# A fourth key tile for VectorE in six odd heads, its bias in the two groups that need it, and fourteen blocks in head 0

## The reference

```
query = x Wd_q Wu_q + rope(x Wd_q Wq_r)      key = x Wd_kv Wu_k + rope(x Wk_r)
value = x Wd_kv Wu_v                          (biases everywhere)
a     = softmax(query key^T / sqrt(272)) value, per head
x1    = layernorm(x + a Wo + b)
y     = round(x1 / s) (int8, s from the largest |x1|) times an int8 matrix, scaled, + bias
out   = layernorm(x1 + y)
```

## Time and profile before

| what | value |
|---|---|
| median of 3 runs | 1922.75 us (1921.45 to 1923.99) |
| profiled execution | 1922.54 us, its span 1920.7 us |
| busy share of the span | PE 96%, PEld 23%, DVE 82%, ACT 94%, POOL 9% |
| instructions of L909 | 1860, busy 1709.7 us |
| granted TensorE clock, mean | 0.99 |

### The profile page before, as it was taken

The page is one execution under the profiler, slowest core; times in us unless marked ns, Lnnn a source line. Parts: engine busy times, 40 slices in busy tenths (PEclk is TensorE's granted clock), DMA queues, the critical chain, the costliest instruction groups (busy, mean ns, idle before and its releaser), DMA issues.

```text
span 1920.7 us, 31434 instructions
## 1 busy us (share of the span) xinstructions
PE 1840.5 (96%) x12988; PEld 446.8 (23%) x12988; DVE 1583.1 (82%) x1502; ACT 1804.4 (94%) x2024; POOL 178.4 (9%) x132
## 2 busy tenths in 40 slices
PE   8989999999999999999999999999999999999965
PEld 3442222221221222222122222222222212221235
DVE  3868979988888887888888888888888888988577
ACT  3479999999999999999999999999999999999956
POOL 5645600000000000000000000000001000500010
PEclk9999999999999999999999999999999999999987
DMA  4534111111111011111121101111121101111012
GB/s 142 167 128 151 20 18 23 26 26 26 26 26 25 17 20 19 23 26 26 25 70 26 26 14 19 20 26 25 26 48 26 25 16 20 17 26 26 1 25 88
DMA packets 161383, 73.41 MB, mean 38 GB/s; under 512 B 129968, under 2 KB 146608, under 8 KB 160752
## 3 DMA queue, kind: packets, MB, share of 16 engines
q1 hardware_dynamic: 158224, 66.79, 15.1%
q10 hardware_dynamic: 3008, 4.53, 0.8%
HBM read 49.13 MB, written 20.84 MB: 36 GB/s over the span
## 4 chain that ended last, share of the span: by engine, by line
ACT 53%; PE 30%; issue 8%; DVE 7%; DMA 1%; POOL 0%; ACTq 0%; DVEq 0%; SPq 0%; POOLq 0%
ACT arena L909 52%; PE PS L708 14%; PE PS L658 9%; PE PS L1196 4%; DVE arena L969 2%; PE PS L749 1%; DVE arena L945 1%; DVE arena L955 1%; PE PS L1344 1%; ACT arena L869 0%; PE PS L1169 0%; DVE bn L837 0%; DVE arena L953 0%; DVE arena L965 0%; DMA arena<-arena 0%
## 5 line engine op out<-in xcount | busy, mean ns | idle before, releaser
L909 ACT ACTIVATE arena<-PS 128x1024 f32<-128x1024 f32 x1860 | 1709.7, 1278 | 10.4 <-PE PS L658 8.5
L708 PE MATMUL PS<-arena,Vh 128*32 128x512 f32 x8192 | 1091.5, 605 | 8.9 <-DVE arena L945 8.9
L658 PE MATMUL PS<-Qst,Kst 49*128 49x512 f16 x4096 | 717.5, 383 | 26.9 <-issue 4.6
L969 DVE SCALAR_TENSOR_TENSOR arena<-arena 128x2048 f32<-128x2048 f32 x282 | 645.5, 2289 | 0.1
L945 DVE TENSOR_SCALAR arena<-PS 128x512 int32<-128x512 f32 x376 | 259.5, 690 | 240.0 <-PE PS L658 235.5
L658 PEld LDWEIGHTS PS<-Qst,Kst 49*128 49x128 f16 x4096 | 183.6, 93 | 1030.6 <-ACT arena L909 982.9
L708 PEld LDWEIGHTS PS<-arena,Vh 128*32 128x32 f32 x8192 | 161.7, 108 | 328.5 <-issue 326.5
L965 DVE SCALAR_TENSOR_TENSOR arena<-arena 128x2048 f32<-128x2048 f32 x94 | 216.5, 2303 | 0.0
L953 DVE TENSOR_SCALAR arena<-arena 128x2048 int32<-128x2048 int32 x94 | 116.9, 1244 | 8.2
L955 DVE TENSOR_SCALAR arena<-arena 128x2048 int32<-128x2048 int32 x94 | 117.9, 1254 | 0.0
L1519 POOL TENSOR_SCALAR nmr<-mv 128x16 f32<-128x16 f32 x1 | 0.3, 263 | 1258.3 <-DVE mv L1698 1258.3
(11 more groups left out here) (120 smaller groups left out, 479.9 us busy)
## 6 DMA issues: line engine op xcount, KB each, us to landing
Qst<-q_halves SPq DMA_DIRECT2D x64, 128.0 KB
Kst<-k_halves SPq DMA_DIRECT2D x64, 128.0 KB
Vh<-head_values SPq DMA_DIRECT2D x30, 256.0 KB, 5.5
k_halves<-parts_or_sums SPq DMA_DIRECT2D x16, 256.0 KB, 3.1
q_halves<-parts_or_sums SPq DMA_DIRECT2D x16, 256.0 KB, 2.6
Qst<-q_halves SPq DMA_DIRECT2D x64, 64.0 KB
Kst<-k_halves SPq DMA_DIRECT2D x64, 64.0 KB
head_values<-arena SPq DMA_DIRECT2D x1, 4096.0 KB, 14.3
```

What stands on the lines that cost most here:

```text
L658: return nc.tensor.matmul(out, Kst[par][low:low + HK + 1, at:at + 128], Qst[par][low:low + HK + 1, j * CH:(j + 1) * CH], start=True, stop= ...
L708: last = nc.tensor.matmul(bank(value_bank(t))[32 * j:32 * j + 32, :], Vh[t % 2][:, kt, :], moving, start=kt == first, stop=kt == last_kt)
L909: nc.scalar.activation(ring(at, k), bank(g % SLOTS * SLOT, k), ACT.Exp, scale=EXP_SCALE).then_inc(a.exp, 1)
L969: last = nc.vector.scalar_tensor_tensor(out=t, in0=t, scalar=POLY[3 - j], in1=power if j == 3 else mantissa, op0=ALU.add, op1=ALU.mult)
```

## The change

It has five parts. (1) Key tile 14 goes to VectorE in heads 3, 7, 11, 15, 27 and 31: 100 tiles instead of 94, and 56 groups instead of 58 in those heads, 1848 in all. Since the values of one parity of heads share a buffer (Vh), tile 14's values and ones are stored times V_SCALE for all odd heads; in the odd heads in which ScalarE keeps tile 14 its two groups stand alone at the head's end and get a bias of -ln(V_SCALE). (2) The blocks are spread anew (BLOCKS_OF): 14 in head 0, 13 in heads 1 to 15 and 24 to 30, 12 in heads 16 to 23, 4 in the last. (3) Before attention three value products stand ahead of the last two query chunks; the key maximum's steps move between VectorE's steps; the table load moves behind first_shifts, into the evacuations; the first three score groups wait for their own banks and go ahead of the bias product; the addition of the output bias (first_sums) stands before the last query chunk's steps; and the wait for all of VectorE's steps at the fifth exponential becomes one for each part. (4) ffn_weights is spread over six blocks. (5) In the last norm GpSimd takes tiles 0 to 5 and 12 to 15 from ScalarE, and the first inverse deviations come two additions later.

```diff
@@ -35,14 +35,25 @@
+FOURTH, FOUR = 14, (3, 7, 11, 15, 27, 31)
+
+
 def by_vector(t):
 
-    return BY_VECTOR if t else FIRST_BY_VECTOR
+    return (FOURTH, *BY_VECTOR) if t in FOUR else BY_VECTOR if t else FIRST_BY_VECTOR
+
+
+def scaled(par):
+
+    return (FOURTH, *BY_VECTOR) if par else BY_VECTOR
 
 
 def head_blocks(t):
 
     low, high = ([kt for kt in half if kt not in by_vector(t)] for half in (range(UPPER), range(UPPER, KT)))
+    if FOURTH in low and t % 2:
+        low = [kt for kt in low if kt != FOURTH] + [FOURTH]
     both = min(len(low), len(high))
...
-FIRST_BLOCKS, FIRST_BLOCK = 13, 11
+FIRST_BLOCKS, FIRST_BLOCK = 14, 11
...
+BLOCKS_OF = [FIRST_BLOCKS] + [13 if t < 16 or t >= 24 else 12 for t in range(1, NT - 1)]
+BLOCKS_OF.append(QB * CYCLES - sum(BLOCKS_OF))
...
-        n = FIRST_BLOCKS if t == 0 else len(BY_VECTOR) * QB
-        n = min(n, QB * CYCLES - len(steps))
+        n = BLOCKS_OF[t]
...
-COPY_AFTER = {FIRST_BLOCKS - 1 + len(BY_VECTOR) * QB * t: t for t in range(NT - 1)}
+COPY_AFTER = {sum(BLOCKS_OF[:t + 1]) - 1: t for t in range(NT - 1)}
...
+EARLY_VALUES = 3
...
     for c in LATE:
+        if c == LATE[2]:
+            order += [("v", 0, n) for n in range(EARLY_VALUES)]
         order += [("p", c, QR_), ("p", c, UQ_), ("p", c, QHI)]
-    return order + [("v", 0, n) for n in range(KT // 2)]
+    return order + [("v", 0, n) for n in range(EARLY_VALUES, KT // 2)]
...
+            for g in range(SLOTS):
+                pe.wait_ge(s_ev, max(DONE[p] for p in PRODUCTS if PRODUCT_BANK[p] // SLOT == g))
+                scores(g)
+            pe.wait_ge(s_ev, len(PRODUCTS))
             bias_out()
-            for g in range(SLOTS):
-                scores(g)
...
+        def norm_by_gpsimd(tiles):
+            for t in tiles:
+                nc.gpsimd.tensor_scalar(Y[:, t, :], Y[:, t, :], rstd[:, t:t + 1], nmr[:, t:t + 1],
+                                        ALU.mult, ALU.add).then_inc(e_fp, 1)
...
-                if g == 4:
-                    act.wait_ge(s_dve, len(STEP))
-                nc.scalar.activation(ring(at, k), bank(g % SLOTS * SLOT, k),
-                                     ACT.Exp, scale=EXP_SCALE).then_inc(a.exp, 1)
+                if 4 <= g < 8:
+                    act.wait_ge(s_dve, STEP["low", LATE[g - 4], "q"])
+                if t % 2 == 1 and blocks[0][0] == FOURTH:
+                    nc.scalar.activation(ring(at, k), bank(g % SLOTS * SLOT, k), ACT.Exp, scale=EXP_SCALE,
+                                         bias=small[:, 9:10]).then_inc(a.exp, 1)
+                else:
+                    nc.scalar.activation(ring(at, k), bank(g % SLOTS * SLOT, k),
+                                         ACT.Exp, scale=EXP_SCALE).then_inc(a.exp, 1)
...
-            for first, end in ((0, 4), (4, 8), (8, 12), (12, 17)):
-                store(e_fa, end, first, end)
-            store(e_fa, 22, 17, 22)
+            store(e_fp, 4, 0, 4)
+            sp.wait_ge(e_fp, 6)
+            store(e_fa, 2, 4, 8)
+            store(e_fa, 6, 8, 12)
+            sp.wait_ge(e_fp, 10)
+            store(e_fa, 7, 12, 17)
+            store(e_fa, 12, 17, 22)
             store(e_fv, 3, 22, 25)
-            store(e_fa, 25, 25, 28)
+            store(e_fa, 15, 25, 28)
             store(e_fv, 6, 28, 31)
-            store(e_fa, 26, 31, KT)
+            store(e_fa, 16, 31, KT)
...
-                if p == ("v", 0, 8):
+                if p == ("v", 0, 10):
                     pe.wait_ge(s_kmax, 5)
...
+                        scales = [V_SCALE if kt in scaled(par) else 1.0 for par in range(2)]
+                        if scales[0] == scales[1]:
+                            last = nc.scalar.activation(V[:, :, kt, :], given, ACT.Copy, scale=scales[0])
+                        else:
+                            for par in range(2):
+                                last = nc.scalar.activation(V[:, par:H:2, kt, :], given[:, par:H:2, :], ACT.Copy, scale=scales[par])
...
-                if p == ("v", 0, 7):
+                if p == ("v", 0, 10):
                     first_shifts()
-            nc.scalar.activation(xs[:, 0:1], small[:, 6:7], ACT.Exp)
+                    nc.scalar.activation(xs[:, 0:1], small[:, 6:7], ACT.Exp)
...
             act.wait_ge(e_rs2, 2)
-            norm_by_scalar(e_fa, range(0, 6))
+            norm_by_scalar(e_fa, range(6, 12))
             act.wait_ge(e_mv2, 22)
             deviation(e_sd2, *BATCHES2[1])
-            norm_by_scalar(e_fa, range(6, 12))
             act.wait_ge(e_rs2, 4)
-            norm_by_scalar(e_fa, range(12, 16))
+            norm_by_scalar(e_fa, range(16, 20))
             act.wait_ge(e_mv2, 28)
             deviation(e_sd2, *BATCHES2[2])
-            norm_by_scalar(e_fa, range(16, 22))
+            norm_by_scalar(e_fa, range(20, 22))
...
+            pool.wait_ge(e_rs2, 2)
+            norm_by_gpsimd(range(0, 6))
+            pool.wait_ge(e_rs2, 4)
+            norm_by_gpsimd(range(12, 16))
...
+            def first_sums():
+
+                nc.vector.memset(sums_ok[:, :], 1.0).then_inc(s_sums, 1)
+                dve.wait_ge(s_bo, 1)
+                nc.vector.tensor_tensor(bo, PS[:, OT * CH:OT * CH + D], bo, ALU.add).then_inc(s_bo2, 1)
...
+                if (name, c, n) == ("low", NCH - 1, "k"):
+                    key_lengths(1)
                 if (name, c, n) == ("low", LATE[0], "q"):
-                    key_lengths(1)
-                if (name, c, n) == ("add", LATE[1], "q"):
                     key_row()
...
+                if (name, c, n) == ("low", LATE[2], "q"):
+                    first_sums()
...
-            hooks.update({40: check_range, 50: ffn_weights})
+            hooks.update({40: check_range})
+            hooks.update({50 + step: lambda step=step: ffn_weights(step) for step in range(6)})
...
-                    if 2 * g == end + 4:
+                    if 2 * g == end + (4 if b else 8):
```

55 lines of the change are left out of this document (29 added, 26 removed).

## The result

The changed kernel takes 1913.89 us (median of 6 runs, 1911.77 to 1917.94), the kernel before 1924.85 in the same comparison; the ratio is 0.9947, with an interval of 0.993 to 0.9965. So it gained 10.2 us (6.7 to 13.5) where 15.5 were forecast. The profiled execution took 1911.77 us, its span is 1910.0.

A forecast was written before the change was run, and what follows sets the result against it. ScalarE's exponentials were taken to bound the attention loop, with TensorE close behind. Start -2.5, loop -10.0 and tail -3.0 made -15.5 us, from 1922.75 to 1907.2; own range 1902 to 1911, wider 1900.5 to 1914.5.

The forecast's parts named there:

- the VectorE rival: Attention loop: VectorE becomes the bound, so the loop gives only -1 us and the total is 1916.2; chance 0.14.
- The twelve exponentials: Attention loop: six tiles moved to VectorE take 12 exponentials of 0.917 us off ScalarE's queue, -11.0 us.
- Head ends: Attention loop: first value products wait for bits at five head ends instead of ten, -3 us, bounds -5 and 0.
- Heads 0 and 1 under GpSimd: Attention loop: VectorE runs late where GpSimd adds the output bias, +2.5 us, bounds 0 and 5.
- Heads 27 and 28: Attention loop: VectorE's work in head 28 is 54.8 us against 53.2, +1 us, bounds 0 and 3.
- Head 3: Attention loop: a short head with the range check and three weight steps, late in places, +0.5 us, bounds 0 and 2.
- The start: Ahead of the loop: first exponential at 119.7 instead of 122.25, -2.5 us, bounds 0 and -3.5; shift-row transfer late next.
- The tail: Last norm: ten tiles go to GpSimd and the stores end sooner, -3.0 us, bounds -3.5 and +9.
- GpSimd's price: Last norm: time GpSimd needs per tile, taken as 0.7 us, up to about 2.8 if blocked; as a rival, chance 0.05.
- the rival in which it holds the stores: Last norm: GpSimd's ten tiles delay the stores, total 1927 at 2.8 us a tile; chance 0.05.
- TensorE as the bound: Attention loop: TensorE sets the pace, so the 12 exponentials bring nothing and the total is 1917.3; chance 0.08.

The follow-up runs named there:

- the second profile: The changed kernel itself run once more, with nothing edited, on the same chip: 1914.42 us, ratio 0.9948 to the kernel before.
- the tiles alone: The kernel before with only the fourth key tile, its blocks spread anew and the weight steps spread: 1923.83 us, ratio 0.9994.
- the kernel with the spreading: The changed kernel with GpSimd's output-bias additions spread over heads 0 to 15 and its FFN-bias additions over heads 28 to 31: 1906.59 us, ratio 0.9906.

## Why the prediction was right or wrong

The direction and the pacemaker were right. The time lies outside the forecast's own range of 1902 to 1911, in the upper end of the wider one of 1900.5 to 1914.5, and nearer to the VectorE rival's 1916.2 than to the forecast. The forecast itself was 6.7 us too low. 1.1 to 2.1 of these are the base: the sum was made against one execution of 1922.54 us and three runs around 1922.75, while the kernel before has a median of 1923.8 to 1924.9 over more runs. The rest is the loop.

- **The twelve exponentials.** -11.0 forecast, -10.9 in the profile. VectorE's count of blocks, its 3.42 us a block and its idle time of 160 us came out.
- **Head ends.** -3 forecast. Heads 2 to 16 gave 1.3, heads 25 to 31 without head 28 gave 2.0 (6.1 - 0.6 against 8.8 - 5.3): -3.3. Right, and by the wait named for it (4 value products instead of 12). Head 17 got such a wait anew and takes 0.9 of it back.
- **Heads 0 and 1 under GpSimd.** +2.5 forecast, +1.8 in the first profile, +5.6 in the second. Head 1 alone is +2.7 in the first, and +4.7 in the second with a half-clock stretch in it; its mechanism is the one named, which spreading the additions shows (4.0 over count down to 1.0). Head 0 is -0.9 and +0.9, and that is the clock at the start, not GpSimd: it doesn't fall with the spreading. The term's size came out in part by luck.
- **Heads 27 and 28: the step that failed.** The text took "+1, bounds 0 and 3"; head 28 alone cost 4.7. Two premises of that term failed. It left GpSimd's additions where they were, 16.8 us into head 28; the change itself brings them to 0.8 us ahead of the head. (They lay in head 28 alone before, not in heads 27 and 28 as the description of the kernel has it.) And it put the shortfall at what the sum of work exceeds the head's length by, 54.8 us by forecast and 56.2 by the profile, while the lateness is decided by the worst spells inside it. TensorE's waits for bits say where: 1.38 us at the first value product, behind the split under the additions; 2.10 at a score block; 0.79 at another behind the second maximum. Counted from exponential to exponential these places are 1.3, 2.3 and 1.0 over the pace, which is nearly all of the 4.7. The longest goes so: the normalisation (L958 to L977), a polynomial blocked to 2.84 us and the first maximum, a reduction of 2.27 (L908), stand one behind another with a single block's bits between them, before the bits that the scores' bank waits for, and TensorE stood 2.10 us there (VectorE's and TensorE's timelines of head 28):

```profile
1632.08 0.69 DVE L984 TENSOR_SCALAR arena<-PS 128x512 int32<-128x512 f32 x1
1632.68 2.84 DVE L1008 SCALAR_TENSOR_TENSOR arena<-arena 128x2048 f32<-128x2048 f32 x1
1635.45 2.27 DVE L908 TENSOR_REDUCE absmax<-arena 128x1 f32<-128x2048 f32 x1
1637.65 0.67 DVE L984 TENSOR_SCALAR arena<-PS 128x512 int32<-128x512 f32 x1
...
1638.38 0.39 PE L678 MATMUL PS<-Qst,Kst 49*128 49x512 f16 x1 [2.10 <-DVE arena L984]
```

- **Heads 17 to 24: nothing was forecast, +2.8 came.** 1.5 of it is the half-clock stretch of head 17. The other 1.3 are there in the second profile too, without such a stretch in these heads, and in none without the tiles once such stretches are taken off. 0.9 of them is the wait of 0.99 us at head 17's first value product, which the kernel before didn't have there: the end of head 16 falls on a tile's first block, right after a split, which is the case that the new turn of head ends was to make rarer. The pauses at the projections only moved from heads 18, 21 and 24 to 17, 20 and 23.
- **Head 3.** +0.5 forecast, +0.2 measured (1.3 to 1.5).
- **The start.** -2.5 forecast, -3.8 in the profile, -4.0 alone by ratio (2.1 to 5.8) with 3.0 in that run's profile. The first exponential was forecast at 119.7; the eleven profiles with the new start have 118.4 to 119.8, so the term was near and the first profile lucky. The transfer is late next, as named. What the text took for fixed moved: in the changed kernel's profile the shift is computed at 111.85 instead of 113.02, and the transfer went out 1.2 us sooner.
- **The tail.** -3.0 forecast. Alone it gave 4.1 us in the profile and 5.0 by ratio, over the text's "no larger than 3.4"; within the change the profile shows 2.1. The tile in head 31 is part of the difference (the tiles alone lengthen the tail from 78.8 to 79.8); taking it out of the kernel with the spreading gave only 0.4, and the rest stays open. GpSimd's price was the open one, 0.7 taken, 0.54 measured; the rival in which it holds the stores has no support. The Trainium skill (SBUF — State Buffer, Who interferes with whom) had the tail's VectorE work leave GpSimd alone; 0.54 us a tile, the same for all ten, agrees. The text's bounds for this term don't fit each other: at 2.8 us a tile it has +9 in one place and 17 us late in another, and 0.69 plus a step of 2.28 is 2.97, not 2.8. Nothing hangs on it, since the price came out at the low end.
- **The rivals.** TensorE as the bound is refuted: exponentials taken away shortened the kernel by 9 us by ratio once GpSimd was spread. VectorE as the bound was right in place, heads 1 and 28, and between the forecast and its own figure in size: +6.0 over the count, where the forecast had +1.0 and the rival 10. The text lets GpSimd block the polynomial's last three steps; all four have two inputs in SBUF, and the first (L1004) took 2.78 us instead of 2.30 beside the additions.

In one sentence: the change gives VectorE one block more in 24 heads, while GpSimd's additions take their toll in a few and, in head 28, now fall on its start; it is in those, 1 and 28 above all, that the work doesn't fit, and they, the wait at head 17's first value product and the clock behind TensorE's pauses gave back more than half of what the tiles took (6.0 of 10.9 us in the profile).

## What to carry to other kernels

An engine with idle time to spare in the sum can be full in the few stages in which another engine blocks it: check a new load against the worst stage, and there against the longest spell between two things that others wait for. Work that hangs on a count of other work moves when the count changes: look where it lands before the sum is made. Side work without a deadline, here 48 bias additions, should lie a little in each stage, and it is worth moving just when the engine beside it is loaded more; before that it shows nothing. Where medians of one kernel scatter more than an edit brings, sort the runs by the granted clock before an edit is blamed or praised.
